# Orthogonal convolution in the frequency domain: inverse transform split by the parity of k1, shorter elimination, update products streamed twice

## The chip, the cores and the metric

The kernel runs on one core of one Trainium2 chip. Its time is the device time of one execution in microseconds; three runs of the kernel before took 2893.61, 2900.13 and 2914.12 us, a median of 2900.13. Most executions of a kernel agree within 0.3%.

## The reference

The input x is 32 images of 128 channels of 32 x 32 in float32, the weight 128 x 127 x 3 x 3. The output is x plus a convolution of the group-normalized x whose matrices are made orthogonal, frequency by frequency:

```python
xp = jnp.pad(x, ((0, 0), (0, 0), (PAD, PAD), (PAD, PAD)))     # 34 x 34
xfft = jnp.fft.rfft2(xp, norm='ortho')                         # 34 x 18 frequencies (k1, k2)
vfft = jnp.fft.rfft2(weight, s=(n, n), norm='ortho')           # per frequency V, 128 x 127
wfft = vH @ vfft + eps * eye
ortho = I - 2.0 * (vfft @ jnp.linalg.solve(wfft, vH))          # 128 x 128, per frequency
zfft = W @ xfft
z = jnp.fft.irfft2(zfft, norm='ortho')[:, :, PAD:-PAD, PAD:-PAD] + bias[:, None, None]
x = x + z                                                      # z of _gn(x), groups of 4 channels
```

Because of the symmetry of real data 580 frequencies are solved, in 145 quads of four.

## The kernel before

Four phases stand one behind another, with a barrier between them.

1. The matrices of shifted weight products are made (to some 58 us).
2. The forward transform of x, with PE products along w and h (to some 387 us).
3. The solver (to 2628 us). Each frequency's matrix is built from tables (`form`, `pre`), and then inverted in two halves of 64 rows, each by four pivot blocks of B = 16 (LB = 4). The quads lie in five sets, in two groups: group a has sets 0 to 2 (82 quads), group b sets 3 and 4 (63 quads). `order()` writes the order by hand: a `sweep` (a, k) applies pivot block k to all quads of group a; beside it stands a job that needs no pivots of that group (`pre`, `mid`, `final`), so that DVE can eliminate the next pivot blocks. For a sweep, `take` turns the 16 x 16 pivot blocks of up to 128 x 3 frequencies so that a lane of DVE holds them, `eliminate(n)` inverts them in place without pivoting for n sets at once (n = 3 for group a, 2 for b), and `scale` and `place` write the factors for PE. In the sweep itself PE's loop over units of 8 quads is `apply` (L1039, 32x32 weights, 64 columns streamed), `turn_u` (L1048) and `update` (L1060, 32x128 weights, 64 columns streamed, four quarters of the rows in turn), ACT copies between them, and DVE subtracts the update from the matrix (L1473). A product in float32 shows as two instructions. `mid` couples the halves, `final` multiplies by x's transform and writes the result to `yhat` in HBM through POOL's queue (L959).
4. The inverse (from 2644 us). It works on groups q of BQ = 4 images. SP loads `yhat` into `y_t`, which has two buffers, so the loads of group q wait for the first products of group q-2, and it loads x. Per image PE makes 18 products along k1 (L1562, K = 68: real and imaginary of 34 k1; the same 64 columns are streamed twice), 11 transposes (L1577) and 11 products along k2 (L1589). ACT copies the first products (L1540) and scales x (L1545), DVE copies the transposes (L1610, L1614) and adds to x (L1623), POOL stores the image (L1630).

The order of the y loads is written out by hand. The frequencies lie in `yhat` in blocks of KG = 4 columns k2, k1 outside k2, so rows of a block with consecutive k1 and four k2 are contiguous; a row of 2 KB is four images of 128 channels. The kernel before loads k1 0 to 31 as 32 partitions of 4 rows (`load_y`), k1 32 and 33 of sixteen columns into one partition each (`load_y_rest`), and the two edge columns apart (`load_y_edge`). Those of group 0 are issued in three pieces: two blocks ahead of the loads of the last final job (L919 to L923), two blocks and the rest behind them, the edge behind the barrier.

Of the kernel before, what the change touches and what calls it, by code (L numbers as in the profile page):

```python
# [11 lines left out]
P = 128  # L12
# [3 lines left out]
B = 16  # L16
NP = C // B
# [8 lines left out]
FT_W = 8 * NK2 + 4 * N + 4 * H + HC * H  # L26
# [79 lines left out]
Y_ROWS = [r * N + k1 for lo, hi in ((0, H), (H, N)) for r in range(2) for k1 in range(lo, hi)]  # L106

# [5 lines left out]
def fourier_tables():  # L113
# [9 lines left out]
    i1 = np.zeros((2, 2, N, 2, H))  # L123
# [9 lines left out]
    i1[0, 0, :, 0], i1[0, 1, :, 0] = ch.T, -sh.T  # L133
    i1[0, 0, :, 1], i1[0, 1, :, 1] = sh.T, ch.T
# [3 lines left out]
    i1[1, 0, :, 0], i1[1, 1, :, 0] = half[:, None] * ch.T, -half[:, None] * sh.T  # L138
# [3 lines left out]
    parts = [f1.reshape(P, 4 * NK2 * 2), f2.reshape(P, 4 * N), i1.reshape(2, 2 * N, 2 * H)[:, Y_ROWS].transpose(1, 0, 2).reshape(2 * N, 4 * H),  # L142
             i2.reshape(HC * NK2 * 2, HC * H)]
    out = np.zeros((P, FT_W))
# [71 lines left out]
def build(nc, x, w, bias, fourier, coef, epsc, const, out):  # L216
    ctx = ExitStack()
    with ctx:
# [183 lines left out]
        with ExitStack() as es:  # L402
# [8 lines left out]
            with nc.Block() as block:  # L411
                @block.sync
                def _(sp):
# [6 lines left out]
                    sp.dma_start(tab, fourier).then_inc(s_tab, 16)  # L420
# [277 lines left out]
        i_tab = a(FT_W)  # L698
        i1 = i_tab[0:2 * N, 8 * NK2 + 4 * N:8 * NK2 + 4 * N + 4 * H].rearrange("p (a n) -> p a n", a=2)
        i2 = i_tab[0:HC * NK2 * 2, FT_W - HC * H:]  # L700
        x_in = a(4, HW)
        gs1, gs2 = a(NB), a(NB)
        y_t = a(2, NK2, BQ * C)
        assert a.at - NK2 * BQ * C <= M_AT + (HOME[0] + FIRST[GROUPS[1][0]]) * QUAD * L
# [3 lines left out]
        h_t = a(2, NHC, C)  # L708
        res = a(4, HW)
# [944 lines left out]
```

## Time and profile before

| | |
|---|---|
| median of 3 runs | 2900.13 us |
| profiled execution | 2906.49 us, its span 2904.7 us |
| granted clock of TensorE, mean | 0.907 |
| PE (products) | 2513.5 us busy, 87% |
| DVE | 1924.9 us, 66% |
| ACT | 1391.4 us, 48% |
| POOL | 503.7 us, 17% |
| DMA queue q1 (SP's loads) | 30.5% of 16 engines |
| DMA queue q0 (POOL's stores) | 12.7% of 16 engines |

Times are in microseconds from the span's start. "Busy" is time in which an instruction of that engine ran, so 87% for PE does not say that it ran at its peak; the granted clock is 1.0 at the higher of its two levels (2.4 GHz) and 0.5 at the lower (1.2 GHz). The DMA share is the mean over 16 DMA engines, so one engine that is always at work shows as 6%. A queue is not an engine: q1 holds what SP issued, and its packets are carried by the 16 engines.

### The profile page before, as it was taken

How to read it: one execution, taken by the hardware profiler on the slowest of the kernel's cores; microseconds unless marked ns; L12 is line 12 of the kernel's file. 1: busy time of each engine (PE TensorE's matmuls, PEld its weight loads, DVE VectorE, ACT ScalarE, POOL GpSimd, SP SyncE). 2: the span in 40 equal slices, each digit the busy share in tenths (PEclk: the TensorE clock that was granted, in tenths of full speed). 3: DMA queues.
4: the chain of work that ended last, by engine and by line, in shares of the span. 5: the costliest groups of instructions: out<-in, count | busy, mean ns of one | idle time of the engine just before them, and what ended most of it. 6: DMA issues, size and time to landing. Idle time of an engine off the chain costs nothing. (4 is left out here: it accounts for less than half of the span.)

```text
span 2904.7 us, 88651 instructions
## 1 busy us (share of the span) xinstructions
PE 2513.5 (87%) x37953; PEld 2049.5 (71%) x37953; DVE 1924.9 (66%) x3883; ACT 1391.4 (48%) x3469; POOL 503.7 (17%) x872
## 2 busy tenths in 40 slices
PE   4976967999989999998987978797899898997999
PEld 4954734656565787787875757685777676987998
DVE  6843446887979768595677888886976977001444
ACT  1422422344343566665663646463555663772332
POOL 0012412121310011111110101010312321341000
PEclk7977988999999899999987989897888989997999
DMA  5274485331411274573833345260312314455884
GB/s 190 88 133 85 73 142 160 97 129 58 163 39 41 41 153 90 104 139 75 161 63 76 75 74 100 49 125 24 110 46 73 110 53 128 143 170 121 215 214 139
DMA packets 562597, 309.97 MB, mean 107 GB/s; under 512 B 484616, under 2 KB 495496, under 8 KB 561368
## 3 DMA queue, kind: packets, MB, share of 16 engines
q1 hardware_dynamic: 520896, 183.58, 30.5%
q0 software_dynamic: 41312, 120.73, 12.7%
q8 instruction: 302, 4.95, 0.7%
q14 instruction: 87, 0.71, 0.1%
HBM read 162.85 MB, written 141.30 MB: 105 GB/s over the span
## 5 line engine op out<-in xcount | busy, mean ns | idle before, releaser
L1473 DVE SCALAR_TENSOR_TENSOR arena<-arena,psum 128x512 f32<-128x512 f32 (+2 forms) x608 | 399.0, 719 | 341.4 <-PE psum L1060 341.4
L1434 DVE TENSOR_TENSOR arena<-arena 128x960 f32<-128x960 f32 (+24 forms) x480 | 399.7, 833 | 16.6
L1429 DVE TENSOR_TENSOR arena<-arena 128x960 f32<-128x960 f32 (+8 forms) x600 | 383.0, 688 | 8.2
L1039 PEld LDWEIGHTS psum<-arena 32*32 32x32 f32 x9280 | 170.0, 140 | 224.9 <-issue 223.4
L1060 PE MATMUL psum<-arena 32*128 32x64 f32 x9280 | 314.9, 283 | 13.0 <-ACT arena L1246 9.7
L1060 PEld LDWEIGHTS psum<-arena 32*128 32x128 f32 x9280 | 293.0, 198 | 35.3 <-ACT arena L1246 20.3
L1001 PE MATMUL psum<-arena 128*32 128x256 f32 (+1 forms) x3696 | 262.2, 378 | 40.3 <-DMA arena<-plain 32.3
L1207 ACT COPY arena<-arena 32x128 f32<-32x128 f32 (+2 forms) x608 | 243.8, 401 | 97.2 <-DVE arena L1484 76.0
L1039 PE MATMUL psum<-arena 32*32 32x64 f32 x9280 | 193.6, 238 | 103.8 <-DVEq L1465 95.5
L940 POOL COPY arena<-arena 128x512 f32<-128x512 f32 (+2 forms) x160 | 86.2, 587 | 879.6 <-ACT arena L1207 879.6
L997 PE MATMUL psum<-arena 128*32 128x256 f32 (+1 forms) x2576 | 215.5, 404 | 9.6 <-DVE arena L1473 6.9
L1106 PE MATMUL psum<-arena 128*128 128x160 f32 x1160 | 201.3, 317 | 23.5 <-ACT arena L1286 23.2
L1001 PEld LDWEIGHTS psum<-arena 128*32 128x32 f32 x3696 | 123.2, 111 | 136.5 <-issue 44.2
L1246 ACT COPY arena<-psum 128x512 f32<-128x512 f32 (+2 forms) x152 | 88.0, 579 | 273.8 <-PE psum L1048 273.8
L1106 PEld LDWEIGHTS psum<-arena 128*128 128x128 f32 x1160 | 169.4, 195 | 59.5 <-ACT arena L1286 57.9
L959 POOL DMA_DIRECT2D yhat<-arena x290 | 154.2, 538 | 300.2 <-ACT arena L1322 293.2
L1048 PE MATMUL psum<-arena 128*128 128x512 f32 (+2 forms) x304 | 185.4, 693 | 19.5 <-ACT arena L1240 18.9
L952 POOL DMA_DIRECT2D kept<-arena x145 | 103.0, 710 | 481.3 <-ACT arena L1296 454.8
L1253 ACT COPY arena<-psum 128x512 f32<-128x512 f32 x145 | 85.9, 592 | 169.5 <-PE psum L1001 163.8
L1093 PE MATMUL psum<-arena 128*128 128x96 f32 x1160 | 156.7, 280 | 8.6 <-ACT arena L1278 8.6
L1093 PEld LDWEIGHTS psum<-arena 128*128 128x128 f32 x1160 | 154.0, 199 | 13.7 <-ACT arena L1278 13.7
L1240 ACT COPY arena<-psum 128x512 f32<-128x512 f32 (+2 forms) x152 | 87.8, 577 | 150.9 <-PE psum L1039 149.9
(122 smaller groups left out, 4612.4 us busy)
## 6 DMA issues: line engine op xcount, KB each, us to landing
blocks<-arena POOLq DMA_DIRECT2D x145, 256.0 KB, 2.4
arena<-blocks SPq DMA_DIRECT2D x290, 128.0 KB, 2.8
kept<-arena POOLq DMA_DIRECT2D x145, 256.0 KB, 3.1
arena<-kept SPq DMA_DIRECT2D x145, 256.0 KB, 2.8
xhat<-arena SPq DMA_DIRECT2D x32, 580.0 KB, 15.4
arena<-xhat SPq DMA_DIRECT2D x580, 32.0 KB, 2.6
yhat<-arena POOLq DMA_DIRECT2D x290, 64.0 KB, 2.6
arena<-x SPq DMA_DIRECT2D x8, 2048.0 KB, 9.6
```

Source lines behind the costliest of these rows:

```text
L959: pool.dma_start(yhat[r, QUAD * q:QUAD * q + QUAD, :].rearrange("c (b n) -> (c b) n", n=C), ys[:, m % 2, r, :]).then_inc(S[f"y_stored{m % ...
L997: pe.matmul(columns[quadrant(p)].rearrange("p (a k) n -> p a k n", k=m), K["ident"][:, quadrant(p)], spread(base[:, 0:m, :], 1, n), start= ...
L1001: ins = pe.matmul(columns[quadrant(p), m * a:m * a + m, :], ccoef[:, FREQ[f0 + m * a][0], :], coefs[:, 0:m, L * p:L * p + L], start=not wi ...
L1039: ins = pe.matmul(psum[0][h, L * t:L * t + L], ce[h, sj % NCE, :, slot + t], M[h, home(q) + t, c, :], start=True, stop=True)
L1048: pe.matmul(psum[1][:, 0:L * n], K["nturn"], u_emb[:, u % 2, 0:n].rearrange("p t q r m -> p (t q) r m")[:, :, 0, :], start=True, stop=True ...
L1060: ins = pe.matmul(upd_bank(u, c)[:, L * t:L * t + L], rows.rearrange("p q r m -> p (q r m)"), real_half(rows), start=t == 0, stop=t == n - 1)
L1093: ins = pe.matmul(psum[2][:, 3 * NB * f:3 * NB * f + 3 * NB], emb[:, m % 2, 1, f].rearrange("p q r m -> p (q r m)"), bx[:, m % 3, f, :], s ...
L1106: pe.matmul(banks[:, f // 2, f % 2, :], emb[:, m % 2, 0, f].rearrange("p q r m -> p (q r m)"), work[:, m % 2, f, 0:5 * NB], start=f % 2 == ...
L1207: ins = act.copy(dt[h, t - GROUPS[g][0], :, slot:slot + n].rearrange("p m s -> p s m"), M[h, at:at + n, c, B * piv:B * piv + B])
L1429: ins = dve.tensor_tensor(pr, spread(R[:, t, :, :, j], 3, 2 * w_), both, ALU.mult)
L1434: link(dve.tensor_tensor(rest, rest, pr[:, :, h], op))
L1473: ins = dve.scalar_tensor_tensor(old, old, K["mask"][:, piv:piv + 1], upd_bank(u, c)[:, 0:L * n].rearrange("p (t n) -> p t n", n=L), ALU.m ...
```

## The change

Three parts.

- Inverse. cos and sin at h and h + 17 differ by the sign of (-1)^k1, so products over even and over odd k1, for h = 0 to 16 only, give both halves of the rows as their sum and their difference. `y_t` now has the k1 of one parity for three columns k2 in 102 partitions (3 x real and imaginary x 17), and the table `ie` is block diagonal for the three columns. Per image that makes 12 products with K = 102 and 102 columns in place of 18 with K = 68 and 128. ACT copies the odd half out (`odd_h`), DVE adds and subtracts, and ACT takes over the copies of the transposes. The loads of y become one per column k2 and real or imaginary part: 17 k1 of each parity. The tables of the inverse are loaded apart from those of the forward transform. The PSUM banks are 3, 2 and 3 in place of 2, 2 and 4.
- Elimination. For the first eight of the 16 pivots the lower left 8 x 8 block of the pivot block is no longer updated; the lower right block is updated from the pivot's row, by symmetry.
- Update products of the sweeps. All but a unit's last stream their 64 columns twice, into the place of the next product, which then overwrites the second copy.

```diff
+K3, HN = 3, N // 2
+NE = K3 * 2 * HN
+FT_W = 8 * NK2 + 4 * N
+IT_W = HC * H + 4 * NE
...
+    ie = np.zeros((2, 2, K3, 2, HN, K3, 2, HN))
+    for v in range(2):
+        for parity in range(2):
+            for i in range(K3):
+                ie[v, parity, i, :, :, i] = i1[v * (i > 0), :, parity::2]
...
-        def load_y(sp, q, k):
+        Y_LOADS = 2 * NK2
+        Y_EARLY = KM // K3 * K3
+
+        def load_y(sp, q, k2):
+            kg, at, n = (KG, k2 // KG * KG * N, HN) if k2 < KM else (NK2 - KM, EDGE, (HN + 1) // 2)
             for r in range(2):
-                sp.dma_start(y_t[r * H:r * H + H, q % 2, k:k + KG, :],
-                             yhat[r, k * N:k * N + KG * H, y_cols(q)].rearrange("(n k) c -> n k c", k=KG)).then_inc(s_yl[q % 2], 16)
-
-        def load_y_rest(sp, q):
-            for r in range(2):
-                for n in range(H, N):
-                    row = H * 2 + (N - H) * r + n - H
-                    sp.dma_start(y_t[row:row + 1, q % 2, 0:KM, :].rearrange("n (g k) c -> n g k c", k=KG),
-                                 yhat[r, 0:KM * N, y_cols(q)].rearrange("(g n k) c -> n g k c", n=N, k=KG)[n:n + 1]).then_inc(
-                                     s_yl[q % 2], 16)
-
-        def load_y_edge(sp, q):
-            for r in range(2):
-                for k0, k1 in ((0, KM), (KM, N // 2 + 1)):
-                    sp.dma_start(y_t[r * H + k0:r * H + k1, q % 2, KM:NK2, :],
-                                 yhat[r, EDGE + 2 * k0:EDGE + 2 * k1, y_cols(q)].rearrange("(n k) c -> n k c", k=2)).then_inc(
-                                     s_yl[q % 2], 16)
+                row = (k2 % K3 * 2 + r) * HN
+                sp.dma_start(y_t[row:row + n, q % 2, k2 // K3, :, :],
+                             yhat[r, at:at + 2 * n * kg, y_cols(q)].rearrange("(a b k) c -> k a b c", b=2, k=kg)[k2 % KG]).then_inc(
+                                 s_yl[q % 2], 16)
...
-                                for k in (0, KG):
-                                    load_y(sp, 0, k)
+                                sp.dma_start(i_tab, fourier[:, FT_W:]).then_inc(s_itab, 16)
+                                for k2 in range(2 * KG):
+                                    load_y(sp, 0, k2)
...
-                        load_y(sp, 0, k)
-                    load_y_rest(sp, 0)
+                        for k2 in range(k, min(k + KG, Y_EARLY)):
+                            load_y(sp, 0, k2)
...
-                                ins = pe.matmul(upd_bank(u, c)[:, L * t:L * t + L], rows.rearrange("p q r m -> p (q r m)"),
-                                                real_half(rows), start=t == 0, stop=t == n - 1)
+
+                                m = 1 + (t < n - 1)
+                                ins = pe.matmul(upd_bank(u, c)[:, L * t:L * (t + m)].rearrange("p (a q m) -> p a q m", a=m, q=LB),
+                                                rows.rearrange("p q r m -> p (q r m)"), spread(real_half(rows), 1, m),
+                                                start=True, stop=True)
...
+                            rows = B if j >= HB else HB
...
+                            if j < HB:
+                                for t in range(n):
+                                    for h in range(2):
+                                        both = bass.AP(scaled_row.tensor, scaled_row[:, t, h * w_ + HB - 1 - j:].offset,
+                                                       [lanes, [0, HB], [w_, 2], [1, HB]])
+                                        ins = dve.tensor_tensor(low_prod[:, t, h].rearrange("p (k r) i -> p k r i", r=2),
+                                                                spread(spread(R[:, t, j, h, HB:], 2, 2), 3, HB), both, ALU.mult)
+                                link(ins)
                             link(dve.tensor_copy(R[:, 0:n, j, :, j:], ones))
                             for t in range(n):
-                                at = 4 * w_ * B * t
-                                pr = prod[:, at:at + 4 * w_ * B].rearrange("p (k h x) -> p k h x", k=B, h=2)
+                                at = 4 * w_ * rows * t
+                                pr = prod[:, at:at + 4 * w_ * rows].rearrange("p (h k x) -> p k h x", k=rows, h=2)
                                 both = bass.AP(scaled_row.tensor, scaled_row[:, t, :].offset,
-                                               [lanes, [0, B], [w_, 2], [1, 2 * w_]])
-                                ins = dve.tensor_tensor(pr, spread(R[:, t, :, :, j], 3, 2 * w_), both, ALU.mult)
-                            link(ins)
-                            pr = prod[:, 0:4 * w_ * B * n].rearrange("p (k h r i) -> p k h r i", k=B * n, h=2, r=2)
-                            rest = R[:, 0:n].rearrange("p t k r m -> p (t k) r m")[:, :, :, j + 1:]
-                            for h, op in ((0, ALU.subtract), (1, ALU.add)):
-                                link(dve.tensor_tensor(rest, rest, pr[:, :, h], op))
+                                               [lanes, [0, rows], [w_, 2], [1, 2 * w_]])
+                                ins = dve.tensor_tensor(pr, spread(R[:, t, 0:rows, :, j], 3, 2 * w_), both, ALU.mult)
+                            mark(ins)
+                            made = steps[0]
+                            pr = prod[:, 0:4 * w_ * rows * n].rearrange("p (t h k r i) -> p t h (k r) i", t=n, k=rows, h=2, r=2)
+                            rest = R[:, 0:n, 0:rows, :, j + 1:].rearrange("p t k r i -> p t (k r) i")
+                            if j < HB:
+                                mark(dve.tensor_tensor(low, low, low_prod[:, :, 0], ALU.subtract))
+                            dve.wait_ge(S["chain"], made)
+                            mark(dve.tensor_tensor(rest, rest, pr[:, :, 0], ALU.subtract))
+                            made = steps[0]
+                            if j < HB:
+                                dve.wait_ge(S["chain"], made - 1)
+                                mark(dve.tensor_tensor(low, low, low_prod[:, :, 1], ALU.subtract))
+                            dve.wait_ge(S["chain"], made)
+                            link(dve.tensor_tensor(rest, rest, pr[:, :, 1], ALU.add))
...
-        S1, TB, S2 = psum[0:2], psum[2:4], psum[4:8]
+        S1, TB, S2 = psum[0:3], psum[3:5], psum[5:8]
...
-                        if q:
-                            for k in range(0, KM, KG):
-                                load_y(sp, q, k)
-                            load_y_rest(sp, q)
-                        load_y_edge(sp, q)
+                        for k2 in range(0 if q else Y_EARLY, NK2):
+                            load_y(sp, q, k2)
...
+                            act.copy(odd_h[:, u % 3], S1[u % 3][:, 2 * NE:4 * NE].rearrange("p (k h) -> p h k", h=HN)).then_inc(s_odd, 1)
...
-                            if u >= 2:
-                                pe.wait_ge(s_s1_cp, u - 1)
-                            for i in range(6):
-                                k = 6 * j + i
-
-                                ins = pe.matmul(S1[u % 2][:, i * 2 * H:(i + 2) * 2 * H].rearrange("p (a n) -> p a n", a=2),
-                                                y_t[0:2 * N, q % 2, k, (b % BQ) * C:(b % BQ + 1) * C],
-                                                spread(i1[:, 0 if k < NK2 - 2 else 1, :], 1, 2), start=True, stop=True)
+                                pe.wait_ge(s_yl[q % 2], 16 * Y_LOADS * (q // 2 + 1))
+                            if u >= 3:
+                                pe.wait_ge(s_s1_cp, u - 2)
+                            for e in range(2):
+                                for i in range(2):
+                                    k = 2 * j + i
+                                    ins = pe.matmul(S1[u % 3][:, (2 * e + i) * NE:(2 * e + i + 1) * NE],
+                                                    y_t[0:NE, q % 2, k, e, (b % BQ) * C:(b % BQ + 1) * C],
+                                                    ie[:, 0 if k < NK2 // K3 - 1 else 1, e, :], start=True, stop=True)
...
+                            even = S1[u % 3][:, 0:2 * NE].rearrange("p (k h) -> p h k", h=HN)
+                            odd = odd_h[:, u % 3]
+                            to = along_h[:, b % 2, :, 12 * j:12 * j + 12]
+                            dve.tensor_tensor(to[:, 0:HN], even, odd, ALU.add)
+                            dve.tensor_tensor(to[:, HN:H], even[:, 0:H - HN], odd[:, 0:H - HN],
+                                              ALU.subtract).then_inc(s_s1_cp, 1)
```

In the order fences a row is a line of the file, the operation, what it writes and reads, and the shape it writes; xN stands for N of them in a row.

The SP queue from the last `kept` loads of group a to the second group of the inverse, before the change (`fourier` is the tables, `kept` the parts that the final job reads, `x` the input). L721 is `load_y`, L728 `load_y_rest`, L735 `load_y_edge`.

```order
L721 DMA arena<-yhat 32x4x512 x4
L923 DMA arena<-x 128x1024 x4
L890 DMA arena<-kept 128x512 x63
L721 DMA arena<-yhat 32x4x512 x4
L728 DMA arena<-yhat 1x16x512 x4
L836 UNCONDITIONAL_BRANCH
L1515 UNCONDITIONAL_BRANCH
L735 DMA arena<-yhat 16x2x512
L735 DMA arena<-yhat 2x2x512
L735 DMA arena<-yhat 16x2x512
L735 DMA arena<-yhat 2x2x512
L721 DMA arena<-yhat 32x4x512 x8
```

The same stretch with the change. L737 is the one `load_y` that is left, L892 the `kept` loads, L925 and L1553 the loads of `x`.

```order
L737 DMA arena<-yhat 17x2x512 x16
L925 DMA arena<-x 128x1024 x4
L892 DMA arena<-kept 128x512 x63
L737 DMA arena<-yhat 17x2x512 x14
L838 UNCONDITIONAL_BRANCH
L1542 UNCONDITIONAL_BRANCH
L737 DMA arena<-yhat 17x2x512 x2
L737 DMA arena<-yhat 9x2x512 x4
L737 DMA arena<-yhat 17x2x512 x32
L737 DMA arena<-yhat 9x2x512 x4
L1553 DMA arena<-x 128x1024 x4
```

Ahead of x and of the 63 `kept` loads of the last final job now stand 16 loads of 17 partitions by 2 rows where 4 of 32 by 4 stood. Between that job's loads and the barrier (the two branches) there are 14 instead of 8, behind the barrier 6 instead of 4, and a whole group of the inverse takes 32 + 4 instead of 16.

DVE at the first pivot of an elimination of three sets, before: L1429 makes the products, L1434 is the two updates.

```order
L1414 RECIPROCAL arena<-arena 128x3
L1419 TENSOR_TENSOR arena<-arena 128x3x30
L1421 SCALAR_TENSOR_TENSOR arena<-arena 128x3x15
L1423 COPY arena<-arena 128x3x32
L1429 TENSOR_TENSOR arena<-arena 128x960 x3
L1434 TENSOR_TENSOR arena<-arena 128x96x15 x2
```

And with the change: L1438 is the products of the lower right block, L1453 and L1459 its two updates, L1447, L1455 and L1461 what the upper eight rows still get.

```order
L1424 RECIPROCAL arena<-arena 128x3
L1429 TENSOR_TENSOR arena<-arena 128x3x30
L1431 SCALAR_TENSOR_TENSOR arena<-arena 128x3x15
L1438 TENSOR_TENSOR arena<-arena 128x128 x6
L1441 COPY arena<-arena 128x3x32
L1447 TENSOR_TENSOR arena<-arena 128x8x2x30 x3
L1453 TENSOR_TENSOR arena<-arena 128x3x16x8
L1455 TENSOR_TENSOR arena<-arena 128x3x16x15
L1459 TENSOR_TENSOR arena<-arena 128x3x16x8
L1461 TENSOR_TENSOR arena<-arena 128x3x16x15
```

Three products of 960 elements became six of 128 and three of 8x2x30, and each of the two updates became one of 384 and one of 720 elements; from the ninth pivot on the rows are as before.

## Rows read from the trace of the kernel before

**Rows 1.** Stretches of the span: busy us of each engine with instructions, PEclk the granted clock, then DMA share.

```profile
1489.00:2103.00 614.00, 500.69 (x7568) 422.07 (x7568) 512.48 (x1010) 323.72 (x878) 89.00 (x148) 0.86 0.39 82
2644.00:2905.00 261.00, 253.65 (x2208) 252.96 (x2208) 104.62 (x224) 83.92 (x128) 17.01 (x32) 0.96 0.72 185
```

**Rows 2.** Waits: engine, line, what ended the wait: total us, times, longest.

```profile
PE psum L1039 <- DVEq L1465: 95.5, 10, 19.7
```

**Rows 3.** Stretches of four of the 16 sweeps, columns as in group 1.

```profile
1321.00:1355.00 34.00, 32.64 (x1024) 25.07 (x1019) 19.06 (x28) 19.40 (x41) 2.84 (x5) 1.00 0.12 23
1571.00:1629.00 58.00, 55.53 (x1334) 42.36 (x1334) 33.36 (x54) 25.92 (x59) 4.64 (x8) 0.74 0.01 3
1848.00:1896.00 48.00, 45.56 (x1334) 34.80 (x1334) 33.05 (x53) 27.89 (x61) 4.63 (x8) 0.93 0.01 3
2210.00:2254.00 44.00, 42.30 (x1024) 32.08 (x1024) 19.55 (x29) 19.43 (x41) 3.40 (x6) 0.74 0.05 12
```

**Rows 4.** Chain that ended last, in order of time, two images' first products: start, us, line.

```profile
2853.20 4.08 PE psum L1562 x36
...
2860.84 4.07 PE psum L1562 x36
```

**Rows 5.** Timeline of the SP queue in the inverse: start, us, line, loads.

```profile
2737.20 5.51 SPq L721 DMA_DIRECT2D arena<-yhat  x8
...
2748.10 14.56 SPq L1529 DMA_DIRECT2D arena<-x  x3
```

**Rows 6.** DMA from 61 to 63 us: packets, then queue: packets, MB, share of 16 engines.

```profile
DMA packets 36, 0.26 MB, mean 131 GB/s; under 512 B 4, under 2 KB 4, under 8 KB 4
...
q1 hardware_dynamic: 36, 0.26, 33.2%
```

**Rows 7.** Timeline of the SP queue before that stretch.

```profile
58.39 0.69 SPq L417 DMA_DIRECT2D arena<-shift_mats  x2
```

**Rows 8.** DMA queue q1 from 2617.4 to 2619.6 us, columns as in group 6.

```profile
q1 hardware_dynamic: 28, 0.05, 19.5%
```

**Rows 9.** Timeline of the SP queue before that stretch.

```profile
2608.98 2.47 SPq L721 DMA_DIRECT2D arena<-yhat  x4
2611.50 2.68 SPq L728 DMA_DIRECT2D arena<-yhat  x4
```

**Rows 10.** DMA from 2550 to 2560 us: GB/s in 40 slices, and queue q1.

```profile
GB/s 0 0 0 66 57 25 147 369 377 344 393 402 197 25 25 0 0 0 0 0 164 99 115 238 131 164 180 418 393 361 385 336 156 139 164 0 0 0 0 0
...
q1 hardware_dynamic: 576, 1.05, 33.3%
```

**Rows 11.** DMA queue q1 in the inverse, 2640 to 2900 us.

```profile
q1 hardware_dynamic: 13520, 31.46, 54.4%
```

**Rows 12.** Timeline of DVE in an elimination of three sets (start, us, line, shapes).

```profile
1492.60 3.29 DVE L1429 TENSOR_TENSOR arena<-arena 128x960 f32<-128x960 f32 x3
1495.93 3.35 DVE L1434 TENSOR_TENSOR arena<-arena 128x1440 f32<-128x1440 f32 x2
...
1558.96 0.69 DVE L1429 TENSOR_TENSOR arena<-arena 128x128 f32<-128x128 f32 x3
```

**Rows 13.** Timeline of PE in a sweep: 32x32 and 32x128 weights.

```profile
1873.61 1.16 PE L1039 MATMUL psum<-arena 32*32 32x64 f32 x64
1874.70 2.01 PE L1060 MATMUL psum<-arena 32*128 32x64 f32 x64
```

**Rows 14.** Timeline of PE in a final job: 128x128 weights, 64 columns streamed.

```profile
2097.21 2.00 PE L1125 MATMUL psum<-arena 128*128 128x64 f32 x16
```

**Rows 15.** DMA issues from 2431 to 2436 us: count, KB each, median us to landing.

```profile
arena<-kept SPq DMA_DIRECT2D x7, 256.0 KB, 10.6
```

**Rows 16.** Timeline of the SP queue before the last final job.

```profile
2427.63 2.58 SPq L721 DMA_DIRECT2D arena<-yhat  x4
```

**Rows 17.** Timeline of PE where the last final job begins.

```profile
2468.69 1.22 PE L1116 MATMUL psum<-arena 128*128 128x256 f32 x2 [2.57 <-DVE arena L1473]
```

**Rows 18.** Timeline of PE where the inverse begins.

```profile
2643.96 2.26 PE L1562 MATMUL psum<-arena 68*128 68x128 f32 x9 [16.05 <-DMA arena<-yhat]
```

More of the change, by code:

```diff
@@ L16 @@
 B = 16
+HB = B // 2
 NP = C // B
@@ L141, in fourier_tables @@
         i2[j, :, 0, j], i2[j, :, 1, j] = (cw * weight).T, (-sw * weight).T
[L142 to L144 removed]
+    parts = [f1.reshape(P, 4 * NK2 * 2), f2.reshape(P, 4 * N), i2.reshape(HC * NK2 * 2, HC * H),
+             ie.reshape(4, NE, NE).transpose(1, 0, 2).reshape(NE, 4 * NE)]
+    out = np.zeros((P, FT_W + IT_W))
     at = 0
@@ L1533, in _ @@
                     act.wait_ge(s_aff, 1)
-                    for b in range(NB):
-                        if b >= 2:
-                            act.wait_ge(s_tb, 3 * (b - 1))
-                        for j in range(3):
+                    for it in range(NB + 1):
+                        b = it
+                        for j in range(3 if b < NB else 0):
                             u = 3 * b + j
                             act.wait_ge(s_s1, u + 1)
-                            act.copy(along_h[:, b % 2, :, 12 * j:12 * j + 12],
-                                     S1[u % 2][:, 0:12 * H].rearrange("p (k h) -> p h k", h=H)).then_inc(s_s1_cp, 1)
-                        act.wait_ge(s_xin[b % 4], 16 * (b // 4 + 1))
-                        if b >= 4:
-                            act.wait_ge(s_out[b % 4], 16 * (b // 4))
-                        act.activation(res[:, b % 4, :], x_in[:, b % 4, :], ACT.Identity,
-                                       scale=gs1[:, b:b + 1], bias=gs2[:, b:b + 1]).then_inc(s_lin, 1)
+                            if u >= 3:
+                                act.wait_ge(s_s1_cp, u - 2)
+                            act.copy(odd_h[:, u % 3], S1[u % 3][:, 2 * NE:4 * NE].rearrange("p (k h) -> p h k", h=HN)).then_inc(s_odd, 1)
+                        if b < NB:
+                            act.wait_ge(s_xin[b % 4], 16 * (b // 4 + 1))
+                            if b >= 4:
+                                act.wait_ge(s_out[b % 4], 16 * (b // 4))
+                            act.activation(res[:, b % 4, :], x_in[:, b % 4, :], ACT.Identity,
+                                           scale=gs1[:, b:b + 1], bias=gs2[:, b:b + 1]).then_inc(s_lin, 1)
+                        b = it - 1
+                        for j, (c0, c1) in enumerate(UNITS if b >= 0 else ()):
+                            if b >= 2 and j == 0:
+                                act.wait_ge(s_s2, 3 * (b - 1))
+                            u = 3 * b + j
+                            act.wait_ge(s_tb, u + 1)
+                            full = c1 if c1 < NHC else c1 - 1
+                            ins = act.copy(h_t[0:CW, b % 2, c0:full, :],
+                                           TB[u % 2][0:CW, 0:(full - c0) * C].rearrange("p (k c) -> p k c", c=C))
+                            if full < c1:
+                                n = 2 * NK2 * H - full * CW
+                                ins = act.copy(h_t[0:n, b % 2, full, :], TB[u % 2][0:n, (full - c0) * C:(c1 - c0) * C])
+                            ins.then_inc(s_tb_cp, 1)
@@ new lines, in _ @@
+                    for it in range(NB + 2):
+                        b = it
+                        for j in range(3 if b < NB else 0):
+                            if b >= 2 and j == 0:
+                                dve.wait_ge(s_tb, 3 * (b - 1))
+                            u = 3 * b + j
+                            dve.wait_ge(s_odd, u + 1)
+                            even = S1[u % 3][:, 0:2 * NE].rearrange("p (k h) -> p h k", h=HN)
[4 more added lines that the diff above has]
+                                              ALU.subtract).then_inc(s_s1_cp, 1)
+                        b = it - 2
+                        for j, (c0, c1) in enumerate(UNITS if b >= 0 else ()):
+                            if j == 0:
+                                dve.wait_ge(s_lin, b + 1)
+                            u = 3 * b + j
+                            dve.wait_ge(s_s2, u + 1)
+                            lo, hi = c0 * HC * H, min(HW, c1 * HC * H)
+                            dve.tensor_tensor(res[:, b % 4, lo:hi], S2[u % 3][:, 0:hi - lo],
+                                              res[:, b % 4, lo:hi], ALU.add).then_inc(s_s2_cp, 1)
```

63 lines of the change are left out of this document (20 added, 43 removed).

## The prediction

> **What bounds the kernel now.** On the page PE is busy for 87% of the span, DVE for 66%, and no other engine is near. The stretches show where PE stops [rows 1]: it works for 254 of the 261 us of the inverse, but for 501 of the 614 us around the four middle sweeps of group a. The waits say why: ten times PE waited for DVE's factors, 95.5 us in all, once 19.7 us [rows 2]. Those pauses end in a granted clock of 0.74 in the sweep that follows, where a sweep without one has 0.93 [rows 3]. In the inverse the chain that ended last runs on PE alone: an image takes 7.64 us from first product to first product, 4.07 of them for 36 first-transform products [rows 4], the rest for transposes and second products. PE is the bound. Next the queue that feeds it: SP issues the 16 loads of a group of four images in 10.9 of every 30.5 us [rows 5]. Last the loads themselves, since the change rewrites them: how many of the 16 DMA engines does one load use? Loads of 25 rows of 8 KB fill 33.2% of the 16, 5.3 of them, at 131 GB/s [rows 6], though two had been issued 0.4 us apart [rows 7]: five engines, and the second load stood behind the first on the same five, since ten would show 62%. 25 has the divisors 1 and 5 and no other up to 16. The loads of 16 rows into one partition, which lie in HBM as 4 by 4, leave 19.5%, 3.1 engines, once they are alone [rows 8, 9]. Loads of 128 rows reach 344 to 402 GB/s [rows 10], which is 16 times that of one. So a load seems to use as many engines as a divisor common to both its outer counts allows.
>
> **The y loads, which decide it.** After the change a load of y has 17 partitions (34 rows of 2 KB, strided in HBM), or 9 for the two last columns; the second order fence shows 32 of the first and 4 of the second for a group. 17 and 34 share 17 and 1: one engine, and by [rows 6, 7] the same one each time. Its price: one engine moved 131/5.3 = 25 GB/s [rows 6] and 402/16 = 25 GB/s [rows 10], 82 ns for 2 KB; with pauses the mean is 0.333 x 16 x 10 us / 576 = 92.5 ns [rows 10]. I take 84, near the dense ones. A group puts 32 x 34 + 8 = 1096 rows on that engine: **92.1 us**, where PE needs 25. It also carries a sixteenth of x and of out, 8 rows of 4 KB each per image: 4 x 8 x 0.168 = 5.4 us each. Per group 92.1 + 5.4 + 5.4 = **102.9 us**. Loads of group q+1 are issued while PE works on q, those of q+2 as soon as q is done, so this engine never rests, and nothing of PE, DVE, ACT or of SP's issuing shows behind it. The bounds of the 84: below 78 (26.2 GB/s, if [rows 6] is read as five engines exactly), above 167, the mean of queue q1 in the inverse now, 0.544 x 16 x 260 us / 13520 packets [rows 11], where 16 engines push into few partitions. One engine alone is nearer to [rows 6].
>
> The Trainium skill has such a rule in "DMA: Bandwidth & Descriptors", in the section on why a DMA increments its semaphore by 16: the number of engines is the largest up to 16 that divides the slowest dimension of both sides, the lowest-numbered engines being taken. The trace agrees for 25 rows; by it the loads of 17 come out as above.
>
> **Part by part, against the profiled execution (2906.5 us, its span 2904.7; 0.2% over the median of the runs, 2900.1).**
>
> 1. Elimination on DVE. By [rows 12] an element costs 1.04 ns ((3.29 - 0.69) / (3 x 832)). With three sets and w columns left a pivot has 3 products of 64w elements and 2 updates of 96w: 0.40w us, and 0.72 fixed (3.29 + 3.35 + two gaps of 0.04 at w = 15). For the first eight pivots the change halves these elements and adds 6 products of 128 (2 x 0.69 us) and 2 updates of 384 (0.95): 0.20w + 2.8. Over w = 15 to 8 that is 40.8 us in place of 42.6: **1.75 us** of 72; for two sets, likewise, 1.07. The small instructions eat the rest. PE waits for DVE before the 8 sweeps of group a and one of b: **-15 us**. What could be late next there is nothing: the mid and final jobs end earlier still.
>
> 2. Updates stream twice. Four quarter-row products with 128 weight columns and 64 streamed ones start every (2.01 - 0.27)/15.75 = 0.11 us, the last one's own time taken off; with 32 weight columns the same 64 take (1.16 - 0.21)/15.75 = 0.06 [rows 13]. So the weights set the 0.11, and whole products with 128 weight columns take 4.07/36 = 0.113 us with 128 streamed columns [rows 4] and (2.00 - 0.29)/15 = 0.114 with 64 [rows 14]. The second copy costs **0**, covered by the weight load; bare it would be at most 0.06 us per four for 64 columns more, x 9280/4 x 7/8 = +120 us. In return PE does more in the same time. Sweeps of group a last 48 us, of group b 34; those entered after a pause or falling into a low clock last 58, 56, 44 and 44, and two more 37 (one of each kind in [rows 3]): 44 us over. I take nearly half back, **-20 us** (bounds 0 and -44).
>
>  The skill's "TensorE: Matmul & The Clock Gate" (part 3, what overlaps and what doesn't) lets a weight load overlap a product in flight only where their row groups differ; by it the second copy lies bare, and the sum is 120 us higher. The trace speaks against it: on the whole array 64 and 128 streamed columns take the same time.
>
> 3. End of the solver. The first 16 loads of y stand ahead of x and of the first `kept` loads. Now 4 do, and the kept loads behind them already land 10.6 us after issue [rows 15]: they queue. 16 x 34 = 544 rows on one engine, begun 1.7 us after the issue at 2427.6 [rows 16], end at 2475.0, x at 2480.4, the first kept part at some 2482.5. The last final job began at 2468.7 [rows 17]: +14, less the 35 of points 1 and 2, **-21**. Of the other loads, 14 (issued from 2609.0 [rows 9], then 2588) take 476 x 84 = 40 us and the six after the barrier 6.4: first product of the inverse at 2638, now 2644.0 [rows 18].
>
> 4. Inverse. Group 1's loads run from 2636 to 2636 + 92.1 + 5.4 = 2733.6; groups 2 to 7 take 6 x 102.9 = 617 more, and the last lands at 3352. From the first product of the last group to the end is now 2904.7 - 2860.8 = 44 us [rows 4]; a third fewer first products save 4 x 12 x 0.113 = 5.4, a cold start costs about 8: 47. Span 3399, and 1.8 around it: **3401, say 3400 us.** What the edit saves on PE, 32 x 12 x 0.113 = 43 us, lies behind the loads, as do ACT's added copies and its hand-over of the odd half to DVE.
>
> **The rivals.**
>
> A. The loads spread over all engines, by their 34 rows or by taking engines in turn. For it: all other loads than those of 25 and 16 rows do. Against it: [rows 6 to 8]. An image is then 7.64 - 1.36 = 6.28 us of PE, a group 25.1. SP needs 36 x 0.68 (10.9/16) = 24.5 us to issue a group [rows 5], and some 2 for the landing: an even race that gives back 7 of the 43. Solver -39 (the last sweep counts too), start +1: **2833 us**. It decides from seven engines a load on (1096 x 84 / 7 = 13 us, and 10.8 of x and out, under 25). Chance 0.09.
>
> B. Two engines, if HBM's count of 34 alone decides: 46 + 10.8 = 57 us a group, the first at 2605, the last at 2655 + 341 = 2996, the end at **3045 us**. Against it: 16 rows on one side and 4 on the other show 3.1 engines [rows 8], so both sides count. 0.03.
>
> C. A, with the second copy bare: 2833 + 120 = **2953 us**. Against it: [rows 4, 14]. 0.01.
>
> **How the numbers follow.** Forecast 0.87, A 0.09, B 0.03, C 0.01. 1 ns more per row is 8.8 us (544 + 476 + 76 + 7 x 1096 rows on the path): 78 ns gives 3350, 92.5 gives 3475, and 105, a quarter of the way to the crowded 167, 3585. With the clock's 0 to -44 and an uneven share for x and out, 3290 to 3590 holds nine in ten of the forecast's 0.87, which is eight in ten of all; A and B lie outside. 1% (29 us) is what a measurement tells from no change: faster 0.09, within 1% 0.01, slower 0.90.
>
> **What would show it.** Inverse: q1 at little over 1/16 of the engines and some 60 GB/s in all, where it is 185 now; PE busy a quarter of the time, waiting seven times some 75 us for y; 103 us from group to group. Solver: a pause of some 17 us before the last final job; a three-set elimination of 71 us; 64 update products still in 2.0 us; sweeps after a long pause nearer 52 than 58 us. It is wrong if q1 shows several engines there, if the inverse runs at 6 to 7 us an image, or if update products take over 0.12 us per four.

## The result, and the profile after

The changed kernel takes **3374.65 us** (median of 4 runs, 3372.44 to 3384.01), the kernel before 2896.87 in the same comparison (2888.28 to 2914.12): ratio 1.1637, 95% interval 1.1582 to 1.1692. Forecast were 3400 us and 3290 to 3590. The profiled execution took 3374.36 us, its span 3372.6. The runs of the kernel before, over all comparisons of this document, lie between 2882 and 2930 us; that is a wider spread than the 0.3% of the opening, and differences of some 10 us below are not to be leaned on.

The page of the changed kernel, busy shares of the engines first, then the chain that ended last:

```profile
PE 2464.4 (73%) x37569; PEld 2011.3 (60%) x37569; DVE 1905.9 (57%) x4843; ACT 1428.0 (42%) x3597; POOL 505.1 (15%) x872
...
PE   5959779999989988997797888888697243312334
...
SPq 21%; PE 1%; issue 0%; DMA 0%; DVE 0%; POOL 0%
SPq L737 20%; PE psum L1627 0%; PE psum L1600 0%; SPq L1553 0%; DMA arena<-yhat 0%; PE psum L1615 0%; DVE arena L1635 0%; POOL out L1666 0%; DVE arena L1659 0%
```

Each digit of the second line is PE's busy share, in tenths, of one of 40 slices of the span. It falls to 1 to 4 in the last nine. The chain, which ran on PE before [rows 4], now runs on SP at line 737, the y loads. The waits of PE, for the whole span:

```profile
PE psum L1600 <- DMA arena<-yhat: 524.2, 8, 72.7
PE psum L1041 <- DVEq L1492: 76.1, 10, 17.7
```

The first line is new: eight waits for y, one ahead of each group of four images. The second answers to [rows 2], 95.5 us before. Two stretches follow: the inverse from its first to its last product (it answers to the second of [rows 1]), and the end of the solver. The columns are PE's busy time, granted clock, DMA share and GB/s:

```profile
2623.49:3365.77 742.28, 246.56 (x1824) 0.62 0.17 64
2375.00:2623.00 248.00, 188.54 (x3292) 0.87 0.39 122
```

The inverse takes 742 us against 254, with fewer products, at 64 GB/s. DMA from 2840 to 3340 us shows why (GB/s in 40 slices of 12.5 us, then queue q1):

```profile
GB/s 105 51 25 25 25 65 148 65 105 64 25 25 26 33 181 66 105 65 25 25 25 27 187 66 106 65 25 25 25 25 188 27 104 106 25 25 25 25 183 20
...
q1 hardware_dynamic: 8838, 22.00, 12.3%
```

Between the bursts of x and out, y arrives at **25 GB/s**: one engine's rate [rows 10], though several loads are issued and unfinished. The timeline of the SP queue (start, us, line, loads) gives the period:

```profile
3016.38 100.03 SPq L737 DMA_DIRECT2D arena<-yhat  x36
3116.45 1.88 SPq L1553 DMA_DIRECT2D arena<-x  x4
3118.38 14.95 SPq L737 DMA_DIRECT2D arena<-yhat  x5
```

102.0 us from group to group (3118.38 - 3016.38). PE at the start of one group:

```profile
2819.86 5.45 PE L1600 MATMUL psum<-arena 102*128 102x102 f32 x24 [67.02 <-DMA arena<-yhat]
...
2831.25 2.88 PE L1600 MATMUL psum<-arena 102*128 102x102 f32 x24
```

After 67 us of standing still the 24 instructions of an image's first products take 5.45 us, at the lower clock, and 2.88 one image later, at the higher. At the end of the solver PE's timeline shows, against [rows 17, 18]:

```profile
2435.10 1.19 PE L1121 MATMUL psum<-arena 128*128 128x256 f32 x2 [22.59 <-DMA arena<-kept]
...
2623.49 6.91 PE L1600 MATMUL psum<-arena 102*128 102x102 f32 x31 [28.85 <-DMA arena<-yhat]
```

The last final job waits 22.6 us (2.6 before) behind 16 loads of y, and the inverse waits 28.9 (16.1). Yet both begin earlier than before, 2435 against 2469 and 2623 against 2644: what the solver gained covers that.

### The profile page after: what moved, and what is told of

The parts are those of the page before. It is cut to its first block and busy times, and to the rows that moved or that the text cites. A ratio compares the mean times of both kernels' runs of the same rounds, so it can differ in the third digit from the quotient of the medians.

```text
span 3372.6 us, 89225 instructions
## 1 busy us (share of the span) xinstructions
PE 2464.4 (73%) x37569; PEld 2011.3 (60%) x37569; DVE 1905.9 (57%) x4843; ACT 1428.0 (42%) x3597; POOL 505.1 (15%) x872
## 3 DMA queue, kind: packets, MB, share of 16 engines
q0 software_dynamic: 41312, 120.73, 10.8%
## 5 line engine op out<-in xcount | busy, mean ns | idle before, releaser
L1600 PE MATMUL psum<-arena 102*128 102x102 f32 x768 | 117.3, 323 | 524.2 <-DMA arena<-yhat 524.2
L1600 PEld LDWEIGHTS psum<-arena 102*128 102x128 f32 x768 | 112.6, 236 | 525.6 <-DMA arena<-yhat 496.3
L1649 DVE TENSOR_TENSOR arena<-psum,arena 128x204 f32<-128x204 f32 x96 | 35.7, 371 | 580.5 <-ACT arena L1565 580.4
L1064 PE MATMUL psum<-arena 32*128 32x128 f32 (+1 forms) x9280 | 298.8, 273 | 10.5 <-ACT arena L1251 9.7
L1064 PEld LDWEIGHTS psum<-arena 32*128 32x128 f32 x9280 | 277.9, 186 | 31.8 <-ACT arena L1251 21.0
L1565 ACT COPY arena<-psum 128x204 f32<-128x204 f32 x96 | 31.8, 331 | 614.6 <-PE psum L1600 614.6
L1041 PEld LDWEIGHTS psum<-arena 32*32 32x32 f32 x9280 | 160.9, 137 | 198.1 <-issue 193.6
L1447 DVE TENSOR_TENSOR arena<-arena 128x320 f32<-128x320 f32 (+6 forms) x600 | 260.5, 485 | 8.3
L1041 PE MATMUL psum<-arena 32*32 32x64 f32 x9280 | 183.0, 230 | 85.1 <-DVEq L1492 76.1
L1111 PEld LDWEIGHTS psum<-arena 128*128 128x128 f32 x1160 | 168.9, 195 | 66.1 <-ACT arena L1291 64.7
L1251 ACT COPY arena<-psum 128x512 f32<-128x512 f32 (+2 forms) x152 | 88.1, 579 | 242.1 <-PE psum L1050 242.1
```

Of the source, the lines that this page charges most:

```text
L1041: ins = pe.matmul(psum[0][h, L * t:L * t + L], ce[h, sj % NCE, :, slot + t], M[h, home(q) + t, c, :], start=True, stop=True)
L1064: ins = pe.matmul(upd_bank(u, c)[:, L * t:L * (t + m)].rearrange("p (a q m) -> p a q m", a=m, q=LB), rows.rearrange("p q r m -> p (q r m)" ...
L1111: pe.matmul(banks[:, f // 2, f % 2, :], emb[:, m % 2, 0, f].rearrange("p q r m -> p (q r m)"), work[:, m % 2, f, 0:5 * NB], start=f % 2 == ...
L1447: ins = dve.tensor_tensor(pr, spread(R[:, t, 0:rows, :, j], 3, 2 * w_), both, ALU.mult)
L1600: ins = pe.matmul(S1[u % 3][:, (2 * e + i) * NE:(2 * e + i + 1) * NE], y_t[0:NE, q % 2, k, e, (b % BQ) * C:(b % BQ + 1) * C], ie[:, 0 if k ...
```

## The experiments

**e1_y16, e2_16of17: is it the count of 17?** e1 moves the 17th pair of k1 out of each block, so that loads have 16 partitions (HE is 16); e2 only cuts the loads short: it leaves part of the sum out, and is good for its time alone. The main load of e1, against the change:

```
-                row = (k2 % K3 * 2 + r) * HN
-                sp.dma_start(y_t[row:row + n, q % 2, k2 // K3, :, :],
-                             yhat[r, at:at + 2 * n * kg, y_cols(q)].rearrange("(a b k) c -> k a b c", b=2, k=kg)[k2 % KG]).then_inc(
...
+                for part, a0, n in (((2 * g + r) * HE, 0, HE), (2 * K3 * HE + 2 * g + r, HE, 1)):
+                    sp.dma_start(y_t[part:part + n, q % 2, 0:2 * KG, :],
+                                 rows[2 * KG * a0:2 * KG * (a0 + n)].rearrange("(a n) c -> a n c", n=2 * KG)).then_inc(
...
```

In e2, `HN` in the first line of load_y becomes `HN - 1`.

> The change with its y loads cut so that no load has 17 partitions: the 17th pair of k1 of each column goes to partitions 96 to 101 by loads of its own, the other 16 pairs take 16 partitions, and four columns of a group share one load; 28 loads a group of images in place of 36, the same bytes, all else as in the change. Theory (one engine carries the loads of 17): the inverse becomes PE-bound at some 6.3 us an image, group to group 25 us in place of 102; the pause of 22.6 us before the last final job and 12 of the 29 us before the first product go too: first product at 2591, end of the span at 2591 + 201 + 16 = 2808, time 2810 us (2795 to 2840). Rival (the loads are not what costs, the new hand-over from ACT to DVE or the semaphores are): over 3200 us. Rival (SP's issuing or the 16 queues' share become the bound): 30 us a group, 2850 us.

> The change with the 17th partition of each y load left out (k1 = 32 and 33 are not read: part of the sum is left out), so the same 36 loads a group with 16 partitions in place of 17, 6% fewer rows. Theory (a load uses as many engines as divide both its outer counts): 16 engines, q1 spread over all of them, a group no longer at 102 us but bound by SP's issue of 36 loads at 0.64 us or by PE, 25 to 29 us: 2815 to 2850 us. Rival (the order of addresses or the many short rows make it slow, whatever the number of partitions): a group takes 0.94 of 102 us, 3330 us.

e1: **2853.65 us**, ratio to the kernel before 0.9815 (0.976 to 0.9869). e2: **2821.82 us**, 0.9701 (0.9645 to 0.9756). One partition fewer a load takes 553 us off: the theory holds, and both rivals of over 3200 us fall. e2 lies in its range of 2815 to 2850 us. In e2 SP's issuing is the next bound, as rival A of the prediction had it. Its queue, one group:

```profile
2609.59 25.59 SPq L737 DMA_DIRECT2D arena<-yhat  x36
2635.22 1.89 SPq L1553 DMA_DIRECT2D arena<-x  x4
2637.15 25.60 SPq L737 DMA_DIRECT2D arena<-yhat  x36
```

From group to group it is 27.6 us, where PE needs 25; the inverse takes 221 us. (36 loads took 100 us to issue in the changed kernel, 2.8 each, and 25.6 here, 0.71 each: while the one engine was behind, SP was held as well. A group is 32 loads of 17 partitions and 4 of 9.)

e1 missed its range by 14 us. The last final job starts 2.6 us after the sweep, so that pause is gone, and the first product comes at 2598 us for the 2591 expected. But the inverse takes 260 us in the profile, whose execution (2867 us) is the slowest of its four. The rival in which the 16 queues' share becomes the bound had 2850 us and 30 us a group; the loads of two groups start 30 and 34 us after those of the group ahead, so it is the nearer one. Why that share was used up, e5 shows below. The same stretch, 2640 to 2780 us, of two kernels, PE alone (busy, clock, DMA share, GB/s), of e1 first, then of e2:

```profile
2640.00:2780.00 140.00, 127.98 (x968) 0.84 0.93 211
```

```profile
2640.00:2780.00 140.00, 134.66 (x1162) 0.95 0.77 236
```

e1 keeps the DMA engines busier and moves less. PE's waits of e1 from 2590 us on:

```profile
PE psum L1627 <- DMA arena<-yhat: 19.5, 1, 19.5
PE psum L1642 <- ACT arena L1606: 16.0, 8, 5.4
```

PE has eight small waits for ACT, 16 us. ACT itself stood 19.1 us, in seven waits, until stores of out had landed. Over the whole inverse PE is busy for 244 us at a clock of 0.83.

**e5_spread: why e1's rows were slow.** Only the partition of each row changes; bytes, loads and HBM rows stay. The cut is against e1; its other two load functions change alike.

```
-    ie = np.concatenate([ie[:, :, 0:HN - 1].reshape(4, -1, NE), ie[:, :, HN - 1]], 1)
+    ie = ie.transpose(0, 2, 1, 3)
...
-                for part, a0, n in (((2 * g + r) * HE, 0, HE), (2 * K3 * HE + 2 * g + r, HE, 1)):
-                    sp.dma_start(y_t[part:part + n, q % 2, 0:2 * KG, :],
+                for part, a0, n in ((2 * g + r, 0, HE), (2 * K3 * HE + 2 * g + r, HE, 1)):
+                    sp.dma_start(y_t[part:part + 6 * n - 5:6, q % 2, 0:2 * KG, :],
```

> As e1_y16, but row pair a of block j = 2i + r lies in partition 6a + j in place of 16j + a, so that a load of 16 partitions is spread over 91 of them; bytes, loads and rows in HBM as in e1_y16, whose y rows of 2 KB took 205 to 265 ns at 92% DMA share where PE stood still seven times for ACT and fell to a clock of 0.82. Theory (the 16 engines push into 16 neighbouring partitions, which together take no more than some 110 GB/s): y rows fall to 90 to 130 ns, DMA share under 0.75, PE at 0.95 or more of its clock, the inverse 260 -> 221 us, 2815 us. Rival (the eight neighbouring rows of HBM that one partition takes are the slow side, or the ten larger bursts): rows stay over 200 ns, 2850 us.

**2802.21 us**, ratio 0.9687 (0.962 to 0.9754), the fastest of all: the change's three parts with y loads that spread over engines and partitions. Queue q1 in 10 us in which it carried y rows and none of x, e1 from 2670 and e5 from 2690 us (packets, MB, share):

```profile
q1 hardware_dynamic: 653, 1.03, 78.8%
```

```profile
q1 hardware_dynamic: 1143, 1.87, 74.3%
```

That is 103 GB/s with loads into 16 neighbouring partitions and 187 with loads into 16 that lie six apart, at nearly the same share of the engines. The same stretch as above, of e5:

```profile
2640.00:2780.00 140.00, 139.41 (x1267) 1.00 0.76 245
```

PE hardly stops and keeps its full clock in this stretch. An image takes 6.29 us (7.63 before), and the inverse 208 us, of which PE is busy for 207 at a clock of 0.97; the prediction's rival A had 6.28 us an image and 2833 us. The 13 us that e5 is under what was expected of it lie there, where 221 were expected.

The Trainium skill has this in "SBUF — State Buffer", the section on the DMA port swizzle: bandwidth goes by how many of 16 ports the partitions reach, and 16 neighbouring ones reach four, 109 GB/s by its figure. The trace agrees, with 103. The prediction's range did not need it, since one engine's 25 GB/s lies far below.

**e6_split: the nearest mend.** Each load is cut into 16 and 1 (8 and 1 for the edge columns), nothing else.

```
-                sp.dma_start(y_t[row:row + n, q % 2, k2 // K3, :, :],
...
+                cut = min(n - 1, HN - 1)
+                for a0, a1 in ((0, cut), (cut, n)):
+                    sp.dma_start(y_t[row + a0:row + a1, q % 2, k2 // K3, :, :],
...
```

> The change with each y load cut in two, 16 partitions and the 17th alone (8 and 1 for the two edge columns), the layout as in the change: 72 loads a group in place of 36. Theory (only the count of 17 hurt): DMA no longer bounds, but SP issues 72 loads at 0.64 us, 46 us and 2 for x a group, more than PE's 25: 8 groups from 2605 or so, end at 2605 + 7 x 48 + 44 = 2985, 2985 us (2960 to 3020). Rival (short loads of one partition cost less to issue, 0.3 us): 36 us a group, 2900 us. Rival (one engine after all): 100 us a group, 3350 us.

**2971.7 us**, ratio 1.0256 (1.0205 to 1.0308): inside its range, and slower than before. The loads no longer bound it, SP's issuing does: PE waits seven times for y, 113.8 us. Its queue:

```profile
2686.68 45.09 SPq L739 DMA_DIRECT2D arena<-yhat  x72
2731.82 1.82 SPq L1555 DMA_DIRECT2D arena<-x  x4
2733.69 6.26 SPq L739 DMA_DIRECT2D arena<-yhat  x10
```

A load takes 0.63 us to issue, those of one partition no less, and a group 47.0.

**e3_elim, e4_double, e7_inverse_only: one part each, on the kernel before.** e3 has only the new `eliminate`; e4 only the line with `m = 1 + (t < n - 1)` and its product; e7 only the inverse of e5.

> The kernel before with the elimination of the change alone. In the change a three-set elimination is 2.2 us shorter and a two-set one 1.4, and the waits before the group a sweeps are 20 us shorter in all. Theory S (the second stream raises the granted clock): only the 20 us come, the sweeps of 57, 55, 44, 44 and 41 us stay in the main: 2886 us in the profile. Rival P (the low-clock sweeps came from pauses of 19 us and over, which a shorter elimination brings under that): the two sweeps of 57 and 55 fall to 48 as well, 2868 us.

> The kernel before with the second stream of the update products alone. Theory S: waits before sweeps stay at 95 us, but the sweeps after the long pauses run at 47 to 48 us and those of group b at 34 to 38: sweeps 35 us shorter in all, 2871 us in the profile; 64 update products still in 2.01 us. Rival P: the sweeps after pauses of 19 us and over stay at 55 to 57 us, 10 to 17 us gained in the others, 2892 us. Rival (the copy lies bare): 64 products in 2.9 us and over 3000 us.

> The kernel before with the inverse of e5_spread alone: the elimination and the update products as before. Theory: 33 us of PE (24 first products in place of 36, with ACT and DVE hidden): inverse 254 -> 221 us, 2900 -> 2870 us against the kernel before, ratio 0.988. Rival (with y loads as slow as in e1_y16 nothing is gained): ratio 1.00.

- e3: 2883.53 us, ratio 0.9895 (0.9834 to 0.9957). PE's waits for the factors: 73.8 us. The profiled execution took 2863.57 us with all sweeps at 678 us together, which is nearer to rival P's 2868 than to theory S's 2886; the median is nearer to 2886, so the times do not tell the two apart.
- e4: 2874.77 us, ratio 0.9879 (0.9811 to 0.9947). Waits 94.8 us, as before; all sweeps together 672 us, 702 before; theory S had 667.
- e7: 2866.82 us, ratio 0.9873 (0.9799 to 0.9946). Inverse 207 us from first to last product, 254 before (266 in a second profile of the kernel before, e8, at a clock of 0.92 for 0.96).

Each part alone is a gain of 1.0 to 1.3%. The intervals are clear of 1, by 0.4 to 0.5% at the near end, and none of the three gains reaches 2%.

**e8_before_again, e9_spread_single, e10_spread_oldelim: who raises the clock?** e8 is the kernel before, e9 and e10 are e5 with `m = 1` as before, and with the old `eliminate`.

> The kernel before, unchanged, for a second profile of its solver. If the sweeps of 57, 55, 44, 44 and 41 us belong to the pauses of over 18 us and to the place in the program, they come back in the same sweeps; if the clock falls by chance, other sweeps are long, and what one profile shows of e3_elim and e4_double cannot be told apart sweep by sweep.

> e5_spread with the update products streamed once, as before; elimination and inverse of the change stay. In six profiles with the second stream the four middle sweeps of group a take 190 to 192 us together; with one stream 208, 198 and 208 with the old elimination and 193.5 with the new. Theory S (the stream fills PE's time, so a pause costs less clock): sweeps 10 to 30 us longer in all, waits before them unchanged, 2802 -> 2820 us. Rival P (the short elimination alone had done it): sweeps as in e5_spread, 669 us, 2802 to 2808 us.

> e5_spread with the elimination as before; the second stream and the inverse of the change stay. Theory: the waits of PE before the sweeps come back, 87 -> 104 us, the sweeps stay at 670: 2802 -> 2820 us. Rival P (the clock hangs on the length of the pause as well): two of the middle sweeps of group a at 51 us or more, 2830 us.

e8: 2894.32 us (one run). e9: **2827.65 us** (0.9728, 0.9682 to 0.9774). e10: **2835.59 us** (0.9743, 0.9696 to 0.979). By the medians the second stream is worth 25 us in the fastest version and the elimination 33, but their runs spread over 20 to 30 us, e5 was measured in another comparison, and the three ratios (0.9687, 0.9728, 0.9743) differ by 12 and 16 us only, with intervals that overlap. Both sizes are rough. e10 is 16 us above what was expected of it: its first product of the inverse comes at 2613.8 us for 2585.3 in e5, 20 of those 28 us being the waits before the sweeps and 6 the sweeps, and its inverse takes 3.5 longer. The next fences show the four middle sweeps of group a, which follow the longest pauses (PE's busy us, clock, DMA share, GB/s). e8, one stream, old elimination:

```profile
1566.86:1617.53 50.67, 48.85 (x1334) 0.85 0.02 4
1703.13:1754.72 51.59, 49.31 (x1334) 0.85 0.01 3
1840.46:1888.56 48.10, 45.82 (x1334) 0.92 0.01 3
1974.16:2021.32 47.16, 45.35 (x1334) 0.93 0.01 4
```

e10, two streams, old elimination:

```profile
1566.90:1613.92 47.02, 45.18 (x1334) 0.93 0.02 4
1699.50:1747.56 48.06, 45.78 (x1334) 0.92 0.02 4
1833.16:1881.04 47.88, 45.48 (x1334) 0.93 0.02 3
1966.63:2013.71 47.08, 45.25 (x1334) 0.93 0.01 4
```

Which sweeps are long is not fixed: 57 and 55 us (first and last of the four) in the profile before, 51 and 52 (first and second) in e8, of the same kernel. But over all profiles the four take 208, 198 and 208 us with one stream and the old elimination (before, e8, e7), 193.6 and 193.5 with one stream and the new one (e3, e9), and 190 to 192 in all seven with two streams, whatever the elimination. None of these four is above 49 us in those seven, though in e4 and e10 PE paused up to 21.0 and 20.8 us before one. With the old elimination and the same pauses, then, the stream takes 8 to 18 us off the four. A shorter pause does most of that too, so the rival was partly right, and the two gains overlap.

All 16 sweeps together, in us:

| | one stream | two streams |
|---|---|---|
| old elimination | 702, 676, 699 (before, e8, e7) | 672, 675 (e4, e10) |
| new elimination | 678, 685 (e3, e9) | 666, 671, 673, 669, 668 (the change, e1, e2, e5, e6) |

e9, as theory S had it, is 16 us longer than e5 here. Of the three sweeps of group b before the last, one or two ran at a clock of 0.75 to 0.82 in the kernel before, e3 and e9 (none in e7 and e8), and none below 0.88 in the seven profiles with two streams.

## Why the prediction was right, point by point

- **y loads (decided it): right.** 102.0 us a group for 102.9, 25 GB/s between the bursts, 524 us of waits for y. Where y was alone on its queue a packet of 2 KB lasted 85 to 86 ns (means of 20 us), but where no store ran either, one started every 82, for the 84 of the sum; in stretches with x it lasted 91 to 101 (114 in the last). So 1096 rows are 90 us for 92.1, and x and out 12 for 10.8: two small misses cancel. e2 shows that the 17 does it, since 16 partitions and 6% fewer rows end the wait. That both outer counts matter rests on [rows 6 to 9]; no run varied HBM's count alone. "q1 at little over 1/16" was put too low: 12.3%, as x goes through q1 as well. PE was busy for 33% of the inverse for a quarter, as it ran at the lower clock for much of it, and the seven waits after the first were 71 us each for 75.
- **Elimination: right, sized a fifth too low.** The 15 pivots of a three-set elimination now span 68.65 us from first to last reciprocal, 70.86 before: 2.2 us for 1.75; with two sets 1.4 for 1.07. PE's wait for factors fell by 19.4 us for 15. But the working does not add up: 0.72 fixed, 1.38 for the six products and 0.95 for the two updates are 3.05 us a pivot and not 2.8, and with 3.05 the elimination would have got longer by 0.2 us. That the 2.8 came near is luck as far as the working shows. What the change adds to a pivot measures 2.0 us, where the written terms have 2.33. One part of that: six products take 1.30 us, not 1.38. The updates save as well, as each starts before the one ahead has ended. The timeline of DVE at the first pivot, against [rows 12]:

```profile
464.81 1.30 DVE L1438 TENSOR_TENSOR arena<-arena 128x128 f32<-128x128 f32 x6
...
466.41 1.80 DVE L1447 TENSOR_TENSOR arena<-arena 128x480 f32<-128x480 f32 x3
468.12 0.55 DVE L1453 TENSOR_TENSOR arena<-arena 128x384 f32<-128x384 f32 x1
468.59 0.90 DVE L1455 TENSOR_TENSOR arena<-arena 128x720 f32<-128x720 f32 x1
469.40 0.55 DVE L1459 TENSOR_TENSOR arena<-arena 128x384 f32<-128x384 f32 x1
469.87 0.91 DVE L1461 TENSOR_TENSOR arena<-arena 128x720 f32<-128x720 f32 x1
```

  The gain is not even: the first pivot is 0.98 us shorter, the sixth no longer is, and the eighth is 0.43 longer (spacings of the reciprocals).

- **Second stream: free, as read, and its return sized from too few sweeps.** The rows against [rows 13], PE's timeline of the changed kernel:

```profile
2405.07 1.13 PE L1050 MATMUL psum<-arena 128*128 128x512 f32 x2
2406.13 1.03 PE L1041 MATMUL psum<-arena 32*32 32x64 f32 x56
2407.09 2.01 PE L1064 MATMUL psum<-arena 32*128 32x128 f32 x64
```

  64 products with 128 columns streamed take 2.01 us, as with 64: rival C falls. The sentence of the Trainium skill, in "TensorE: Matmul & The Clock Gate", part 3, that a weight load overlaps a product in flight only where their row groups differ, does not hold here. On the whole array, where all products use the same row groups, they start every 0.11 us with 64 columns as with 128 [rows 4, 14], and in the updates the second copy cost nothing. The sweeps together went from 702 to 666 us, -35 for -20. Part of that is the chosen profile: a second one of the kernel before has 676 (e8). On average over the table above the stream with the old elimination is worth 19 us. The forecast had expected nearer 52 than 58 us in sweeps after a long pause; they took 47 to 49.
- **End of the solver: mechanism right, the first product 14 us earlier than forecast.** The pause before the last final job is 22.6 us for 17. The last sweep ended at 2412.5 us for 2466.1 before, 54 us earlier where points 1 and 2 gave 35; so the first product came at 2623.5 for 2638.
- **Inverse: right.** From the first product of group 1 (2717.7) to that of group 7 (3329.9) 612 us for 617, from there to the end 43 for 47. Of the 26 us that the forecast was too high, 14 are the solver's, 5 the groups', 4 the tail's, and 2 the first group's: it took 94 us from the first product for 96. The tail's are the cold start, put at 8 us with no row behind it: it cost 4 (42.7 us from the last group's first product to the end, 38.7 in e5, whose PE did not stop).
- **Rival A** was sized right as a mechanism: with spread loads and 36 issues (e2) it gives 2822 for 2833, and SP's queue is the bound by 2.5 us a group. It lost because its condition did not hold. Without the issue bound (e5) it is 2802.

**What stays open.** Whether HBM's count matters by itself was not tested. Which engine carried the loads is not in the trace; that successive loads did not take different ones is, by the 25 GB/s. Why a pause in the kernel before is sometimes followed by a clock of 0.74 and sometimes by 0.93 was not found.

## What to carry to other kernels

Before a layout is changed, count what each transfer's outer sizes share: 17 partitions put 32 loads a group on one engine and cost 553 us, more than ten times what the edit saved on TensorE. Then count issues (0.63 to 0.71 us each on the SP queue here): the split into 16 and 1 mends the engines and loses to the queue. And when a profile shows pauses before slow stretches, streaming idle columns under a weight load can be worth as much as shortening the pause: 1.2% here against 1.0%, too close to rank.

## What the runs showed of the hardware that was not expected

- SP's issue is not a fixed cost: 0.71 us a load in e2, where the engines keep up, 2.8 us in the changed kernel, where one is behind, so every later load of that queue waits too.
- Loads of y into 16 neighbouring partitions moved 103 GB/s, into 16 partitions six apart 187, at nearly the same busy share of the engines (79% and 74%). With that came waits of PE for ACT of 16 us in all and, over the inverse, a granted clock of 0.83 for 0.97; the waits and the 37 us that PE is busy for longer are the 52 us by which the inverse is longer (260 against 208).
